# Two 64 x 64 matmuls on the diagonal in place of one block-diagonal 128 x 128 matmul

## What is computed

```python
def ffn(x, W_base, b_base, W_enc, b_enc, W_dec, b_dec, W_down, b_down, W_up, b_up, connected_idx):
    # x: 16 x 512 x 256; W_enc: 8 x 256 x 64; W_dec: 8 x 64 x 256
    base = einsum('btd,de->bte', x, W_base) + b_base
    h = relu(einsum('btd,ndh->nbth', x, W_enc) + b_enc[:, None, None, :])
    recon = einsum('nbth,nhd->nbtd', h, W_dec) + b_dec[:, None, None, :]
    losses = mean((recon - x[None]) ** 2, axis=(2, 3))
    top1 = argmin(losses, axis=0)
    adp = connected_idx[top1]
    mid = relu(einsum('btd,bdr->btr', x, W_down[adp]) + b_down[adp][:, None, :])
    return base + einsum('btr,brd->btd', mid, W_up[adp]) + b_up[adp][:, None, :]

x = x + 0.5 * ffn(layernorm(x), ...)
x = x + attention(layernorm(x), ...)
x = x + 0.5 * ffn(layernorm(x), ...)
```

## Time and profile before

| | |
|---|---|
| median of 3 runs | 1784.11 us (1783.69 to 1787.06) |
| the profiled execution, time | 1784.44 us |
| the profiled execution, span from first to last instruction | 1782.6 us |
| TensorE busy with matmuls (PE) | 1703.6 us, 96% |
| TensorE busy with weight loads (PEld) | 997.6 us, 56% |
| VectorE (DVE), ScalarE (ACT), GpSimd (POOL) busy | 71%, 55%, 28% |
| mean granted TensorE clock | 0.988 of full speed |

### The profile page before, as it was taken

How to read it: one execution, slowest core, us unless ns; L and a number is a source line. 1 busy time by engine, 2 the same in 40 slices (tenths; PEclk the granted TensorE clock), 3 DMA queues, 4 the chain that set the end, 5 groups by cost and what they waited for, 6 DMA issues and landing times.

```text
span 1782.6 us, 26353 instructions
## 1 busy us (share of the span) xinstructions
PE 1703.6 (96%) x9064; PEld 997.6 (56%) x9064; DVE 1265.2 (71%) x2829; ACT 973.0 (55%) x1954; POOL 497.0 (28%) x663
## 2 busy tenths in 40 slices
PE   5878999999999999999999999999999999999987
PEld 4624555556565565656556565655656565554345
DVE  6478786867768686776868677686867868576722
ACT  2326474655637465563746556474655647465551
POOL 2314060421406042140604215060421506023010
PEclk9889999999999999999999999999999999999999
DMA  5343342223334222343422234332233434224300
GB/s 133 48 71 72 37 82 32 62 40 60 72 49 79 35 61 42 61 72 48 76 36 62 43 61 72 48 75 36 61 45 60 72 48 75 32 33 70 44 1 24
DMA packets 96715, 99.37 MB, mean 56 GB/s; under 512 B 19972, under 2 KB 88261, under 8 KB 96453
## 3 DMA queue, kind: packets, MB, share of 16 engines
q1 hardware_dynamic: 93830, 97.16, 32.6%
q10 hardware_dynamic: 2752, 0.54, 0.2%
HBM read 63.54 MB, written 33.55 MB: 54 GB/s over the span
## 4 chain that ended last, share of the span: by engine, by line
PE 84%; DVE 8%; ACT 2%; issue 2%; POOL 2%; DMA 1%; SPq 0%; POOLq 0%; ACTq 0%; DVEq 0%
PE ps L1706 11%; PE ps L1692 11%; PE ps L1680 11%; PE ps L1778 10%; PE ps L1761 10%; PE ps L1780 6%; PE ps L1821 5%; PE ps L1837 5%; PE ps L1822 3%; PE ps L1802 3%; PE ps L1745 2%; PE ps L1847 2%; DVE mx L2076 2%; PE ps L1884 2%; PE ps L1868 2%
## 5 line engine op out<-in xcount | busy, mean ns | idle before, releaser
L2076 DVE TENSOR_REDUCE mx<-ps 128x1 f32<-128x512 f32 x1024 | 655.5, 683 | 258.8 <-PE ps L1680 257.6
L1919 ACT ACTIVATE pr<-ps 128x512 f32<-128x512 f32 x1024 | 557.3, 599 | 386.5 <-PE ps L1692 383.0
L1680 PE MATMUL ps<-stack 96*128 96x512 bf16 x1024 | 316.0, 384 | 12.4 <-DVE mx L2076 8.5
L1692 PE MATMUL ps<-stack 98*128 98x512 bf16 x1024 | 314.6, 384 | 9.2 <-ACT pr L1919 3.3
L1706 PE MATMUL ps<-pr,va 128*32 128x512 f32 x2048 | 247.7, 602 | 2.6 <-ACT pr L1919 2.3
L1692 PEld LDWEIGHTS ps<-stack 98*128 98x128 bf16 x1024 | 82.4, 98 | 184.5 <-issue 106.9
L1680 PEld LDWEIGHTS ps<-stack 96*128 96x128 bf16 x1024 | 95.2, 98 | 156.0 <-DVE mx L2076 50.9
L2321 POOL CAST wdh<-wd_all 128x128 fp32r x32 | 9.5, 297 | 585.2 <-DVE adapter L2165 557.4
L2131 DVE SCALAR_TENSOR_TENSOR ps<-ps,wb,h 128x512 f32<-128x512 f32 x128 | 96.5, 755 | 65.1 <-PE ps L1780 65.1
L1780 PE MATMUL ps<-h,gram_w 128*128 128x512 f32 x256 | 130.6, 592 | 0.0
L1706 PEld LDWEIGHTS ps<-pr,va 128*32 128x32 f32 x2048 | 53.7, 109 | 136.2 <-issue 131.2
(11 more groups left out here) (153 smaller groups left out, 2951.5 us busy)
## 6 DMA issues: line engine op xcount, KB each, us to landing
stack<-scratch SPq DMA_DIRECT2D x384, 128.0 KB, 6.3
scratch<-parts SPq DMA_DIRECT2D x64, 384.0 KB, 2.6
xin<-in_L_attn_x_dram SPq DMA_DIRECT2D x15, 512.0 KB, 4.0
out_dram<-x SPq DMA_DIRECT2D x15, 512.0 KB, 8.8
stack<-wu_mT SPq DMA_DIRECT2D x128, 4.0 KB, 1.7
cst<-in_const_dram SPq DMA_DIRECT2D x1, 1024.0 KB
raw<-in_L_ffn_W_dec_dram ACTq DMA_DIRECT2D x1, 512.0 KB, 5.6
pr<-in_L_ffn_W_enc_dram SPq DMA_DIRECT2D x2, 256.0 KB, 7.6
```

Of the source, the lines that this page charges most:

```text
L1680: pe.matmul(bank1[:, t % 2, :], stack[0][0:KB, hd, 128 * t:128 * t + 128], stack[1][0:KB, hd, :], start=True, stop=True).then_inc(s1_full. ...
L1692: pe.matmul(bank2[:, a % 2, :], stack[1][:, 4 * g + a, 128 * t:128 * t + 128], stack[0][:, 4 * g + a, :], start=True, stop=True).then_inc( ...
L1919: act.activation(held(b, n)[:, a, :], bank2[:, a % 2, :], ACT.Exp, scale=SCALE).then_inc(ex_done.sem, 1)
L2076: dve.tensor_reduce(mx[:, hd // 4 % 2, e:e + 1], bank1[:, t % 2, :], AX.X, ALU.max).then_inc(mx_done.sem, 1)
```

## The change

In the gram stage the last call, one fp32 matmul of a 128 x 128 stationary matrix with 512 columns of h, becomes two calls. The first takes rows 0 to 63 of gram_w's block and of h and writes partitions 0 to 63 of the bank; the second takes rows 64 to 127 and writes partitions 64 to 127. The zero blocks are no longer multiplied. The signal to VectorE is on the second call. R is 64.

```diff
@@ -1777,7 +1777,9 @@
                     for w, x in ((w_dh, xh), (w_dl, xh), (w_dh, xl)):
                         pe.matmul(bank, w[:, c, 128 * p:128 * p + 128], x[e][:, c, :],
                                   start=(c == 0 and w is w_dh and x is xh), stop=False)
-                pe.matmul(bank, gram_w[:, p, :], h[:, p, :], start=False, stop=True).then_inc(gr_full[f].sem, 1)
+                for q in (slice(0, R), slice(R, 2 * R)):
+                    last = pe.matmul(bank[q], gram_w[q, p, q], h[q, p, :], start=False, stop=True)
+                last.then_inc(gr_full[f].sem, 1)
```

## The result

| | before | changed |
|---|---|---|
| median, us | 1784.01 (1783.69 to 1787.06, 4 runs) | 1817.91 (1815.68 to 1820.7, 4 runs) |
| profiled execution: time and span, us | 1784.44, 1782.6 | 1819.96, 1818.1 |

The changed kernel is slower: ratio 1.0187, 95% interval 1.0166 to 1.0208, or 33.9 us. Forecast were 1813 us and a range of 1793 to 1828.

The account below looks back on a forecast made before the run. TensorE, busy for 96% of the span, was taken as the bound. 128 grams x 0.24 = 30.7, -1.2 for pv, -2 hidden in waits, +1 for exposed loads: +28.5 on 1784.4 gave 1813 us, range 1793 to 1828.

Parts of the forecast that it names:

- Side by side, nothing to win: Gram's last call: the two 64*64 corners run together in two rounds, 0.86 us as now, so streaming gains nothing.
- Three or four rounds: Rivals at the gram: passes queue in order, three rounds, 1868 us, 6%; corners not side by side, four, 1924, 5%.
- the rival of the cheaper 64-row pass: Rival at the gram: half the rows let an fp32 pass run in 0.21 us; -24, 1760 us; chance 3%.
- The price of the division: At each gram: 0.09 us going in, exposed weights 0.02 + 0.03, 0.10 coming out; 1.33 against 1.09, +0.24.
- the sum: Per gram 1.33 against 1.09 us; for the kernel 128 x 0.24 = 30.7, -1.2, -2, +1: +28.5.
- One change shared with pv: In each of 13 turns one gram is followed by pv, which already pays 0.09 for changing division: -1.2 us.
- What waits hide: Only the 0.10 of coming out can hide, in VectorE's wait, at one or two grams a turn: -2 us.

Follow-up runs that it names:

- the run with rows alone: Kernel before, the gram's last call made one call over the upper 64 rows, all 128 columns, lower rows' product left out: 1820.51 us against 1786.38, ratio 1.0192.
- The run with columns alone: Kernel before, the gram's last call made two calls of 128 rows by 64 columns, nothing left out: 1811.89 us against 1786.38, ratio 1.0168.

## Why the prediction was right, and where its size was off

*Side by side, nothing to win.* Right: two rounds of two, 0.48 apart. Three or four rounds aren't there, and the rival of the cheaper 64-row pass is refuted by the run with rows alone. The Trainium skill (TensorE: Matmul & The Clock Gate, Part 3, The mechanism) has matmuls start in strict program order. Two passes to a call and two starts at 906.79 and again at 907.27 don't fit that, if a call's two passes are issued together; how they are issued no profile row shows.

*The price of the division.* Right in kind and size: 0.09 going in, 0.05 of exposed weights, 0.10 coming out, 1.33 against 1.09. One term was 0.01 small: the sum took 0.22, the distance between bf16 matmuls, for the last fp32r one, whose own is 0.23, and so had 0.31 ahead of the first pass in place of 0.32. That it is the form, and not the count of instructions, the division of rows rather than columns, or the place in the sequence, is shown by the runs above. The Trainium skill (TensorEngine Tiling (Array Packing), Key Properties) says a change of tiling mode drains the engine; the gaps on both sides (0.09 and 0.10), and the loads that wait for them (0.05), agree. The fp32r call of 64 columns shows no such gap (0.23 ahead, 0.24 behind).

*One change shared with pv.* Right: in the changed kernel, too, a gram with pv behind it hands over in 0.52:

```profile
935.63 1.08 PE L1781 MATMUL ps<-h,gram_w 64*64 64x512 f32 x4
936.64 0.64 PE L1706 MATMUL ps<-pr,va 128*32 128x512 f32 x4
```

From the first pass to pv it is 1.01, as it is to s2 (906.79 to 907.80); in the kernel before it is 0.95 to pv and 0.86 to s2. So a change between two divided forms costs what one to the whole array does, and such a gram loses 0.09 less.

*What waits hide.* The forecast took 2 us off. Between the pv at 125.13 and the one at 1661.65 of the kernel before there are 112 grams, and the shift goes from 4.72 to 29.59:

```profile
125.13 1.07 PE L1706 MATMUL ps<-pr,va 128*32 128x512 f32 x8
1661.65 1.07 PE L1706 MATMUL ps<-pr,va 128*32 128x512 f32 x8
```
```profile
129.85 1.06 PE L1706 MATMUL ps<-pr,va 128*32 128x512 f32 x8
1691.24 1.06 PE L1706 MATMUL ps<-pr,va 128*32 128x512 f32 x8
```

24.9 us, where 112 x 0.24 less 1.2 for pv is 25.7: about 1 us hidden. The steady part is as forecast.

*What the sum left out.* Forecast +28.5, measured +33.9 (the profiled pair: +35.5). Beyond the 24.9, 4.7 us arise ahead of 129.85 and 5.9 behind 1691.24, with eight grams each, worth 2 to 3. Most of the rest is the clock. At the start the same weight loads of the preparation, ahead of any gram, take 1.8 times as long in the changed kernel's execution. First the kernel before, then the changed one:

```profile
16.66 0.53 PEld L1902 LDWEIGHTS ps<-raw 128*128 128x128 f32 x4
```
```profile
16.33 0.97 PEld L1904 LDWEIGHTS ps<-raw 128*128 128x128 f32 x4
```

The first encoder matmul starts 3.0 later for it (21.52 against 18.48). The trace's first record of the granted clock, at the full level, stands at 15.5 us in the kernel before and at 23.6 in the changed one; for the time ahead of it the views print 1.00, though none is recorded. In the other nine traces it stands between 13.7 and 16.1, at 14.7 in the run with the same two calls ahead of the fp32r ones. At the end the 32 matmuls of the last stage up, up to the end of the span, take 2.55 us longer, at a granted clock of 0.65 in place of 0.86 (busy time by window, columns as in the earlier trace rows):

```profile
1773.70:1782.60 8.90, 4.83 (x32) 4.26 (x32) 1.38 (x2) 0.00 (x0) 0.00 (x0) 0.86 0.17 59
```
```profile
1806.65:1818.10 11.45, 7.38 (x32) 6.56 (x32) 1.38 (x2) 0.00 (x0) 0.00 (x0) 0.65 0.14 46
```

The part at the start is no effect of the change, as it comes before the first gram. Whether that at the end is one wasn't tried. Near its end the changed kernel's trace has a stretch of 10.2 us at the lower level, the kernel before one of 3.4; four of the other nine have one of 10.2 as well, the undivided fp32r gram among them. The changed kernel's four times, 1815.68 to 1820.7, spread by more than this part. So the term that was missing is the clock at the two ends, some 5.5 us of the profiled 35.5, which the sum took as equal. The run with columns alone bears this out: its grams cost as much (1.34), its first record of the clock stands at 15.4, and its profiled execution is 27.4 us over that of the kernel before, 1 below the forecast for the corners. One of the four changed executions is the profiled one; how much of the clock's part the other three have, whose traces aren't kept, stays open.

*A version that beats both.* The gram in fp32r, undivided, at 1722.13 us is 3.5% below the kernel before, because one pass of 0.23 takes the place of two of 0.43. 128 x 0.63 would be 80 us; 62 arrived, and where the rest stayed wasn't traced. It rounds h and the matrix, so the losses that choose the adapter are coarser. It isn't a way of dividing the array; it shows that the cost of this call was its two slow passes, and not its zero blocks.

## What to carry to other kernels

Multiplying zeros cost nothing here, as the number of streamed columns stays the same: a block-diagonal matrix should be split over the array only if the parts replace calls that now stream one after the other. Each stretch in a divided form cost about 0.2 us of an otherwise dense TensorE stream (0.09 in, 0.10 out) plus the weights that weren't loaded ahead, so divided calls belong together, as pv's eight do. On a TensorE that is busy for 96% this went to the end time almost in full.

## What the runs showed of the hardware

- A change of form costs 0.09 us on entry whether rows, columns or both are divided, in fp32, and also in fp32r if the rows are divided (0.32 or 0.33 ahead in each, 0.23 undivided). An fp32r call of all 128 rows and 64 columns at column 0 costs nothing (0.23 ahead, 0.24 behind); the same call in fp32 does (0.32 ahead).
- The first round's exposed weight load grows with the columns: rounds of 0.45, 0.48 and 0.53 us for 32, 64 and 128 columns, where 0.43 is the covered one.
- Eight matmul records of four fp32 calls in four column tiles (1007.18 and 1007.63), or four of two calls in two corners (906.79 and 907.27), run as two rounds. That each tile's second pass waits without holding up the other tiles fits these starts; no row names the tile of a record.
- Doubling instructions and loads in the undivided form cost 0.01 us a gram (1.10 against 1.09), and nothing that could be measured in all.
